# Value products two blocks of exponentials behind, and the side steps that move with them

## The chip, the cores and the metric

The kernel runs on one core of one Trainium2 chip. The metric is the device time of a launch in microseconds (us). The engines named below are TensorE (PE; its weight loads are PEld), VectorE (DVE), ScalarE (ACT), GpSimd (POOL) and SyncE (SP), which here only starts DMAs. Each engine works through its own list of instructions in order and waits on semaphores that others raise.

## The reference

The input x is 32 sequences of 128 rows by 512 columns, float32. The first layer is cross attention with 8 heads of 16 dimensions over the 512 columns, the second a mixture of experts.

```python
q = proj(x1t, Wq, bq); k = proj(x2t, Wk, bk); v = proj(x2t, Wv, bv)
scores = einsum('bhqd,bhkd->bhqk', q, k) / sqrt(D_HEAD)
attn = softmax(scores, axis=-1)
out = einsum('bhqk,bhkd->bhqd', attn, v)
x = x + tanh(g_xattn[0]) * xattn(layernorm(x), ctx)
# rmsnorm, router (8 experts, the best 2), gate/up/down of 256, one shared expert
x = x + tanh(g_ffn[0]) * ffn(layernorm(x))
```

## The kernel before, in words

One sequence, b, has 512 positions. For each of the 8 heads the 512 keys are cut into 4 tiles of 128, which gives 32 steps (STEPS) a sequence, each with a score tile of 128 keys by 512 queries. The attention stage is a loop over turns i = -3 to 31; each engine's list holds the same turns, and a turn has 32 steps in 8 blocks of 4 (GROUP). The order is written out by hand: constants such as PROJECT_AT, VALUES_LATE and LOGITS_AT (lines 35 to 43) say at which step a side job stands in each engine's list.

In turn i TensorE does, block by block (line 969 on): four matmuls of scores of sequence i+1 for the row maxima (max_scores, L838), which VectorE reduces two at a time (maximum, L1089, two pairs of PSUM banks); two score tiles of sequence i (exp_scores, L860); one group of four value products (values, eight matmuls in float32, L890); two more score tiles. ScalarE takes the exponential of each score tile (L1351) into one of three probs buffers of four tiles each. The score tiles, and also the projections, turned maxima, turned tokens and router logits, share three PSUM banks in rotation (take_bank): a bank's next user waits for the reader of its last content.

The value products of one sequence are eight groups r. Group r takes the probs of block r. Groups 0 to 3 add up in one PSUM bank, pv_ps, then ScalarE copies it out (take_values, L1366), and groups 4 to 7 add up in the same bank and are copied out as well. The product of a half's first group therefore waits for the copy of the half before (line 888). In the kernel before, group r is issued one block behind its exponentials: at step s, group s/4 - 1, and group 7 in the first block of the next turn. take_values stands at step VALUES_LATE + 1 = 4 (second half of sequence i-1) and 20 (first half of i) of ScalarE's list.

The copied bank holds numerators and the sums of exponentials (denominators). SyncE spreads the denominators over partitions (spread_denominators, L454), VectorE inverts them (invert, L1081, at step RECIP_AT), SyncE stores and reloads the reciprocals (L458, L464), and GpSimd multiplies, gates and adds to x (add_attention, L655 to L657). One turn later VectorE takes moments (moments2), GpSimd normalises into the single buffer tok (tokens, L676 to L690, which waits for the turning of the tokens before), and one more turn later TensorE turns it (turn_tokens, L865), ScalarE copies it (take_turned, L1373), and TensorE makes router logits (router_logits, L877). The negated row maxima go from ScalarE (take_maxima, L1358) by one DMA for each half into the q stack (row, L498), where the score tiles of that half need them.

After turn 31 come 103 jobs of the expert stage, which starts when TensorE's list has ended the attention.

Of the kernel before, what the change touches and what calls it, by code (L numbers as in the profile page):

```python
# [31 lines left out]
COLUMNS = tuple(slice(c, c + 2 * DH) for c in range(0, P, 2 * DH))  # L32
STEPS = HEADS * KT

PROJECT_AT = {24: (3, 0), 28: (3, 1), 8: (2, 2)}
EVAC_AT = {27: (3, 0), 31: (3, 1), 11: (2, 2)}
MAX_AT = (19, 3)
VALUES_LATE = 3
TURN_TOKENS_AT = 12
LOGITS_AT = 16  # L40
MOMENTS2_AT = 10
MOMENTS_AT = 27
RECIP_AT = 12
GROUP = 4
EXPERTS = 8
FF = 256
# [34 lines left out]
def build(nc, x_d, ctx_d, g_xattn_d, g_ffn_d, wq_d, bq_d, wk_d, bk_d, wv_d, bv_d, rms_d, router_d, w_d, out_d):  # L81
    B = x_d.shape[0]
# [5 lines left out]
    with es:  # L88
# [291 lines left out]
        def is_b(b):  # L380
            return 0 <= b < B
# [9 lines left out]
        def _(sp):  # L391
# [33 lines left out]
            def copy_parts(b, n, part):  # L425
                if part == HI:
                    if n == 0:
                        if b >= 3:
                            sp.wait_ge(s_es, STEPS * (b - 2))
                        if b < 3:  # L430
                            sp.wait_ge(s_blank[b], 1)
                    sp.wait_ge(s_hi, 2 * b + n + 1)
                if part == LOW:
                    sp.wait_ge(s_part, 2 * b + n + 1)
                stack, src = (k_stack, q_stack)[n][b % 3], parts[n][part]
                for at, slot in enumerate(SLOTS_OF[n]):
                    if slot == part:
                        for a in range(2):
                            rows = stack[LANE * a + at:LANE * a + at + STACK - 2:len(SLOTS_OF[n]), :, :]
                            sp.dma_start(rows.bitcast(F32), src[a:P:2, :].bitcast(F32)).then_inc(s_cp[n], DMA)  # L440
# [8 lines left out]
            def spread_denominators(b):  # L449
                sp.wait_ge(s_u, 2 * b + 2)  # L450
                if b:
                    sp.wait_ge(s_rc, b)
                for g in range(2):
                    sp.dma_start(den_c[P // 2 * g:P // 2 * (g + 1), :], pv_sb[1:P:2 * DH, g, :]).then_inc(s_sc, DMA)  # L454
# [40 lines left out]
            def row(b, half):  # L495
                sp.wait_ge(s_mr, 2 * b + half + 1)
                pairs = slice(half * GROUP // 2, (half + 1) * GROUP // 2)
                sp.dma_start(q_stack[b % 3][STACK:STACK + LANE + 1:LANE, pairs, :].bitcast(F32), m_rows[half].bitcast(F32)  # L498
                             ).then_inc(s_row[half], DMA)

            for i in TURNS:
                if is_b(i + 2):
                    copy_parts(i + 2, 0, HI)
                if is_b(i - 1):
                    spread_denominators(i - 1)
                if is_b(i):
                    row(i, 1)
                if is_b(i + 2):
                    copy_parts(i + 2, 0, LOW)
                if is_b(i - 1):  # L510
                    send_values(i - 1)
                if is_b(i + 2):
                    copy_parts(i + 2, 1, HI)
                if is_b(i - 1):
                    store_reciprocals(i - 1)
                if is_b(i + 2):
                    copy_parts(i + 2, 1, LOW)
                if is_b(i - 1):
                    load_reciprocals(i - 1)
                if is_b(i + 1):  # L520
                    row(i + 1, 0)
                if is_b(i + 4) and i + 4 >= 2:
                    load_ctx(i + 4)
                if is_b(i - 3):
                    store_turned(i - 3)
                if i >= 0 and is_b(i + X_AHEAD):
                    load_x(i + X_AHEAD)
                if is_b(i - 2):
                    store_tokens(i - 2)
                if i < 0:  # L530
                    load_x(i + X_AHEAD)
                if 0 <= i + 2 < len(STAGED):
                    store_staged(i + 2)
                if 0 <= i + 3 < len(STAGED):
                    load_staged(i + 3)
                for r in SHARED_ROWS.get(i, ()):
                    if r == 2:
                        sp.wait_ge(s_sst, DMA * len(STAGED))
                    if r == 0:
                        sp.wait_ge(s_wsh, (W_ROWS - 1) * DMA)  # L540
                    sp.dma_start(w_shared[:, r, :], w_d[0, :, r, :]).then_inc(s_wsh, DMA)
                if i == B - 2:
                    source(0)
                if i == -1:
                    sp.wait_ge(s_spare, 2)
                    map_tiles = map_d.rearrange("(n s) k -> n s k", s=P)
                    for n in range(0, EXPERTS * B, P):
                        sp.dma_start(map_tiles[n:n + P], slot_map[:]).then_inc(s_map0, DMA)
                    sp.dma_start(map_tiles[EXPERTS * B:], unused_map).then_inc(s_map0, DMA)
                if i == 0:  # L550
                    sp.dma_start(w_router[:], router_d.rearrange("(c p) e -> p c e", p=P)).then_inc(s_wnorm, DMA)
# [235 lines left out]
        def _(pe):  # L787
# [93 lines left out]
            def values(b, r):  # L881
                g, kt = divmod(r, KT)
                pair = 8 * b + r
                pe.wait_ge(s_exp, STEPS * b + GROUP * (r + 1))
                if r == 0:
                    pe.wait_ge(s_evac, 3 * b + 3)
                if kt == 0 and pair:
                    pe.wait_ge(s_u, pair // KT)
                for j in range(GROUP):
                    last = nc.tensor.matmul(pv_ps[2 * DH * j:2 * DH * (j + 1), :], v_ones[b % 3][:, kt, GROUP * g + j, :],  # L890
                                            probs[pair % 3][:, j, :], start=(kt == 0), stop=(kt == KT - 1))
                last.then_inc(s_pv, 1)
# [76 lines left out]
            for i in TURNS:  # L969
                for s in range(0, STEPS, GROUP):  # L970
                    if is_b(i + 1):
                        max_scores(i + 1, s)
                        max_scores(i + 1, s + 2)
                    if is_b(i):
                        exp_scores(i, s)
                        exp_scores(i, s + 1)
                    if s == 0 and is_b(i - 1):
                        values(i - 1, STEPS // GROUP - 1)
                    if s and is_b(i):
                        values(i, s // GROUP - 1)  # L980
                    if is_b(i):
                        exp_scores(i, s + 2)
                        exp_scores(i, s + 3)
                    if s + 3 == MAX_AT[1] and is_b(i):
                        turn_maxima(i, 1)
                    if s + 3 == MAX_AT[0] and is_b(i + 1):
                        turn_maxima(i + 1, 0)
                    if s == TURN_TOKENS_AT and is_b(i - 3):
                        turn_tokens(i - 3)
                    if s == LOGITS_AT and is_b(i - 3):  # L990
                        router_logits(i - 3)
                    if s in PROJECT_AT and is_b(i + PROJECT_AT[s][0]):
                        project(i + PROJECT_AT[s][0], PROJECT_AT[s][1])
                    if s + 3 == COUNT_SLOT and i > CHUNK and (i - 3) % CHUNK == 0:
                        count_choices((i - 3) // CHUNK - 1)
                    if i == B - 1 and s == FIRST_JOB_AT:
                        gate_up(0)

            values(B - 1, STEPS // GROUP - 1)

            for j in range(JOBS + 1):
                if j in ROUTER_JOBS:
# [19 lines left out]
        def _(dve):  # L1022
# [171 lines left out]
            for i in TURNS:  # L1194
                for s in range(STEPS):
                    if s % 2 == 0 and is_b(i + 1):
                        maximum(i + 1, s)
                    if s == RECIP_AT and is_b(i - 1):
                        invert(i - 1)
                    if s == MOMENTS_AT and is_b(i + 5):  # L1200
                        begun.append(moments(i + 5))
                    if s == MOMENTS2_AT and is_b(i - 2):
                        begun.append(moments2(i - 2))
                    if s == LOGITS_AT + 3 and is_b(i - 3):
                        take_logits(i - 3)
# [124 lines left out]
        def _(act_e):  # L1330
# [48 lines left out]
            for i in TURNS:  # L1379
# [3 lines left out]
                for s in range(STEPS):  # L1383
# [6 lines left out]
                    if s == EXP_SLOT and i > CHUNK and (i - 3) % CHUNK == 0:  # L1390
                        exponentials((i - 3) // CHUNK - 1)
                    if s == TURN_TOKENS_AT + 3 and is_b(i - 3):
                        take_turned(i - 3)
                    if s == VALUES_LATE + 1 and is_b(i - 1):
                        take_values(i - 1, 1)
                    if s == STEPS // 2 + VALUES_LATE + 1 and is_b(i):
                        take_values(i, 0)
                    if s in EVAC_AT and is_b(i + EVAC_AT[s][0]):
                        evacuate(i + EVAC_AT[s][0], EVAC_AT[s][1])

# [103 lines left out]
```

## Time and profile before

| | us |
|---|---|
| median of 3 runs (1446.69 to 1449.7) | 1448.16 |
| the profiled execution | 1446.75 |
| its span, first to last instruction | 1444.9 |
| TensorE busy | 1319.2 (91%) |
| VectorE busy | 889.8 (62%) |
| ScalarE busy | 853.4 (59%) |
| GpSimd busy | 730.8 (51%) |
| mean granted clock of TensorE, of full speed | 0.968 |

Busy time is the union of an engine's instructions; one that waits for nothing is no bound. Idle time is given beside the instruction that ended it and what released it. A row with xN merges N instructions that follow each other, so a wait inside such a row shows as a longer row and not as idle time. The starts and lengths of matmuls overlap by some hundredths of a us.

### The profile page before, as it was taken

The page shows a single profiled execution, that of the slowest core. Times are in us where ns is not written, and L with a number is a line of the kernel's source. Part 1 is how long each engine was busy: PE and PEld are TensorE (multiplying, and loading weights), DVE is VectorE, ACT ScalarE, POOL GpSimd, SP SyncE. Part 2 cuts the span into 40 slices and gives each one's busy share as a digit, 9 for nine tenths or more (in the row PEclk, how much of TensorE's full clock was granted, in tenths as well). Part 3 has the DMA queues.
Part 4 walks back from the last instruction along what each step waited for, and adds up shares of the span by engine and source line. Part 5 has one row for each costly group of instructions (what it writes and reads, how often), then busy time and mean ns, then how long its engine had stood idle before and what let it go on. Part 6 is the DMA issues. An engine that isn't in the chain of part 4 may idle for free.

```text
span 1444.9 us, 27029 instructions
## 1 busy us (share of the span) xinstructions
PE 1319.2 (91%) x9190; PEld 716.7 (50%) x9190; DVE 889.8 (62%) x1176; ACT 853.4 (59%) x1684; POOL 730.8 (51%) x978
## 2 busy tenths in 40 slices
PE   5989998998998998899999988899899999999997
PEld 2333333333333333333333333387678888888886
DVE  6777777777777778877777776256554333333332
ACT  1677777777777777777777776533234433333332
POOL 7445555545555555546776552120732555555553
PEclk7899999999999999999999998699999999999999
DMA  6555455545545544544665651164963898786665
GB/s 177 151 125 171 149 135 152 156 134 146 162 134 142 163 134 141 169 126 119 148 157 122 140 124 47 64 208 139 105 165 91 190 216 211 180 195 113 109 111 81
DMA packets 123841, 205.84 MB, mean 142 GB/s; under 512 B 28005, under 2 KB 29676, under 8 KB 123710
## 3 DMA queue, kind: packets, MB, share of 16 engines
q1 hardware_dynamic: 105454, 166.74, 42.9%
q0 software_dynamic: 18256, 37.38, 14.1%
q8 instruction: 79, 1.29, 0.4%
q14 instruction: 52, 0.43, 0.1%
HBM read 82.34 MB, written 61.94 MB: 100 GB/s over the span
## 4 chain that ended last, share of the span: by engine, by line
PE 72%; issue 9%; ACT 8%; DVE 4%; DMA 4%; POOL 2%; POOLq 1%; SPq 0%; ACTq 0%; DVEq 0%
PE m_banks L933 20%; PE bank L890 18%; PE bank L860 14%; PE m_banks L838 9%; ACT arena L1351 4%; PE bank L815 4%; PE bank L865 3%; DVE row_max L1089 2%; DMA arena<-ht_d 2%; PE bank L821 2%; ACT arena L1366 2%; POOL xs L757 1%; PE bank L955 1%; PE bank L877 1%; DMA out<-xs,arena 1%
## 5 line engine op out<-in xcount | busy, mean ns | idle before, releaser
L1089 DVE TENSOR_REDUCE row_max<-m_banks 128x2 f32<-128x1024 f32 x512 | 605.9, 1216 | 181.9 <-PE m_banks L838 181.0
L1351 ACT ACTIVATE arena<-bank 128x512 f32<-128x512 f32 x1024 | 557.1, 598 | 227.4 <-PE bank L860 226.5
L890 PE MATMUL bank<-arena 128*32 128x512 f32 x2048 | 284.0, 627 | 70.0 <-ACT arena L1366 68.8
L860 PE MATMUL bank<-q_stack,k_stack 49*128 49x512 f32 x1024 | 285.4, 472 | 2.2 <-ACT arena L1351 2.0
L860 PEld LDWEIGHTS bank<-q_stack,k_stack 49*128 49x128 f32 x1024 | 123.4, 189 | 277.9 <-issue 162.5
L838 PE MATMUL m_banks<-k_stack,q_stack 48*128 48x512 f32 x1024 | 195.9, 456 | 7.3 <-DVE row_max L1089 7.2
L769 POOL DMA_INDIRECT out<-xs,arena x71 | 112.6, 1586 | 159.8 <-ACT xs L1429 121.8
L933 PE MATMUL m_banks<-w_ring,h_hi 128*128 x568 | 183.1, 403 | 0.0
L1418 ACT ACTIVATE arena<-m_banks 128x256 f32<-128x256 f32 x103 | 39.5, 384 | 183.3 <-PE m_banks L933 183.3
L838 PEld LDWEIGHTS m_banks<-k_stack,q_stack 48*128 48x128 f32 x1024 | 90.2, 191 | 98.5 <-issue 68.0
L890 PEld LDWEIGHTS bank<-arena 128*32 128x32 f32 x2048 | 42.6, 109 | 156.2 <-ACT arena L1351 114.3
L933 PE MATMUL m_banks<-w_ring,h_lo 128*128 x284 | 111.7, 393 | 0.0
L933 PEld LDWEIGHTS m_banks<-w_ring,h_hi 128*128 128x128 f32 x568 | 101.4, 189 | 18.4
L1282 DVE TENSOR_TENSOR arena<-arena,m_banks 128x256 f32<-128x256 f32 x71 | 29.9, 421 | 115.7 <-ACT arena L1418 115.7
L712 POOL DMA_INDIRECT map_d<-meta,slots x64 | 64.5, 1008 | 64.8 <-DVE slots L1165 46.4
L1429 ACT ACTIVATE xs<-m_banks,arena 128x512 f32<-128x512 f32 x71 | 48.8, 687 | 71.0 <-PE m_banks L933 71.0
L678 POOL TENSOR_SCALAR arg<-mv 128x1 f32<-128x1 f32 x32 | 6.2, 192 | 166.1 <-DVE mv L1061 166.1
L1276 DVE TENSOR_TENSOR act_lo<-bank,act_hi 128x256 fp32r<-128x256 f32 x71 | 30.1, 424 | 96.6 <-ACT act_hi L1435 96.6
L933 PE MATMUL m_banks<-w_ring,act_hi 128*128 x284 | 87.5, 389 | 1.4 <-DVE act_lo L1276 1.4
L646 POOL CAST arena<-arena 128x512 fp32r<-128x512 f32 x62 | 37.8, 609 | 97.3 <-ACT arena L1338 96.4
L757 POOL DMA_INDIRECT xs<-h_d,arena x71 | 69.7, 981 | 33.3 <-issue 21.0
L815 PE MATMUL bank<-arena 128*32 128x512 f32 x512 | 72.8, 643 | 12.5 <-POOL arena L638 7.7
(175 smaller groups left out, 1795.0 us busy)
## 6 DMA issues: line engine op xcount, KB each, us to landing
k_stack<-arena SPq DMA_DIRECT2D x192, 128.0 KB
q_stack<-arena SPq DMA_DIRECT2D x192, 128.0 KB
split_d<-staged SPq DMA_DIRECT2D x30, 512.0 KB, 5.1
w_ring<-split_d SPq DMA_DIRECT2D x60, 256.0 KB
arena<-in_w SPq DMA_DIRECT2D x36, 256.0 KB, 7.5
arena<-in_ctx SPq DMA_DIRECT2D x32, 256.0 KB, 3.2
xs<-in_x SPq DMA_DIRECT2D x32, 256.0 KB, 4.0
arena<-arena SPq DMA_DIRECT2D x64, 128.0 KB, 3.2
```

The source lines that it names most:

```text
L712: nc.gpsimd.indirect_dma_start(map_d, bass.IndirectOffsetOnAxis(ap=slots[:, k, b:b + 1], axis=0), meta[:, k, b, :], None).then_inc(s_sc2, DMA)
L757: nc.gpsimd.indirect_dma_start(gathered[i % IN_RING], None, h_d, bass.IndirectOffsetOnAxis(ap=ids[:, i:i + 1], axis=0)).then_inc(s_got[i % ...
L769: nc.gpsimd.indirect_dma_start(out_d, bass.IndirectOffsetOnAxis(ap=ids[:, i:i + 1], axis=0), y_sb[i % OUT_RING], None, compute_op=ALU.add) ...
L815: last = nc.tensor.matmul(out[c, :], (wk, wq)[n][:, c], ctx_in[b % 2] if n == 0 else xn[b % 2], start=True, stop=True)
L838: nc.tensor.matmul(m_ps[pair % M_PAIRS][:, a, :], q_stack[b % 3][rows, h, qt * P:(qt + 1) * P], k_stack[b % 3][rows, h, :], start=True, st ...
L860: nc.tensor.matmul(out, k_stack[b % 3][rows, h, kt * P:(kt + 1) * P], q_stack[b % 3][rows, h, :], start=True, stop=True).then_inc(s_es, 1)
L865: last = nc.tensor.transpose(out[:, c * P:(c + 1) * P], src[:, c * P:(c + 1) * P], ident[:])
L890: last = nc.tensor.matmul(pv_ps[2 * DH * j:2 * DH * (j + 1), :], v_ones[b % 3][:, kt, GROUP * g + j, :], probs[pair % 3][:, j, :], start=( ...
L933: last = nc.tensor.matmul(out, v[:, c, :], weights(j, part, first_row + c), start=(c == 0 and n == 0), stop=(c == chunks - 1 and n == 2))
L1089: nc.vector.reduce_max(pair, m_ps[(STEPS * b + u) // 2 % M_PAIRS], AX_X).then_inc(s_mx, 1)
L1351: nc.scalar.activation(probs[group % 3][:, j, :], bank_of["scores", b, s], ACT.Exp, scale=float(DH) ** -0.5).then_inc(s_exp, 1)
L1429: nc.scalar.activation(y_sb[i % OUT_RING], Y_PS[j % 2], ACT.Copy, scale=wts[:, i:i + 1]).then_inc(s_yrt, 1)
```

## The change

The value products move from one block behind their exponentials to two: at step s of turn i TensorE issues group s/4 - 2, and in the first two blocks of a turn groups 6 and 7 of the sequence before. After the loop two groups are left instead of one. VALUES_LATE goes from 3 to 5, so take_values stands at steps 6 and 22. The third projection (values of sequence i+2) moves from step 8 to 12 and its evacuation from 11 to 15. The turned tokens go from step 12 to 4 (copied by ScalarE at 7 instead of 15), the router logits from 16 to 8 (copied by VectorE at 11 instead of 19). The reciprocals move from step 12 to 14. In SyncE's list the row of maxima of the second half goes ahead of the denominators.

```diff
--- before.py
+++ after.py
@@ -32,15 +32,15 @@
 COLUMNS = tuple(slice(c, c + 2 * DH) for c in range(0, P, 2 * DH))
 STEPS = HEADS * KT
 
-PROJECT_AT = {24: (3, 0), 28: (3, 1), 8: (2, 2)}
-EVAC_AT = {27: (3, 0), 31: (3, 1), 11: (2, 2)}
+PROJECT_AT = {24: (3, 0), 28: (3, 1), 12: (2, 2)}
+EVAC_AT = {27: (3, 0), 31: (3, 1), 15: (2, 2)}
 MAX_AT = (19, 3)
-VALUES_LATE = 3
-TURN_TOKENS_AT = 12
-LOGITS_AT = 16
+VALUES_LATE = 5
+TURN_TOKENS_AT = 4
+LOGITS_AT = 8
 MOMENTS2_AT = 10
 MOMENTS_AT = 27
-RECIP_AT = 12
+RECIP_AT = 14
 GROUP = 4
 EXPERTS = 8
 FF = 256
@@ -501,10 +501,10 @@
             for i in TURNS:
                 if is_b(i + 2):
                     copy_parts(i + 2, 0, HI)
+                if is_b(i):
+                    row(i, 1)
                 if is_b(i - 1):
                     spread_denominators(i - 1)
-                if is_b(i):
-                    row(i, 1)
                 if is_b(i + 2):
                     copy_parts(i + 2, 0, LOW)
                 if is_b(i - 1):
@@ -974,10 +974,10 @@
                     if is_b(i):
                         exp_scores(i, s)
                         exp_scores(i, s + 1)
-                    if s == 0 and is_b(i - 1):
-                        values(i - 1, STEPS // GROUP - 1)
-                    if s and is_b(i):
-                        values(i, s // GROUP - 1)
+                    if s < 2 * GROUP and is_b(i - 1):
+                        values(i - 1, STEPS // GROUP - 2 + s // GROUP)
+                    if s >= 2 * GROUP and is_b(i):
+                        values(i, s // GROUP - 2)
                     if is_b(i):
                         exp_scores(i, s + 2)
                         exp_scores(i, s + 3)
@@ -996,7 +996,8 @@
                     if i == B - 1 and s == FIRST_JOB_AT:
                         gate_up(0)
 
-            values(B - 1, STEPS // GROUP - 1)
+            for r in range(STEPS // GROUP - 2, STEPS // GROUP):
+                values(B - 1, r)
 
             for j in range(JOBS + 1):
                 if j in ROUTER_JOBS:
```

## Rows read from the trace of the kernel before

**Rows 1.** The page, parts 1 and 2: busy time, and TensorE's clock

```profile
PE 1319.2 (91%) x9190; PEld 716.7 (50%) x9190; DVE 889.8 (62%) x1176; ACT 853.4 (59%) x1684; POOL 730.8 (51%) x978
...
PEclk7899999999999999999999998699999999999999
```

**Rows 2.** Waits of the whole span: us in total, times, longest us

```profile
PE bank L890 <- ACT arena L1366: 68.8, 63, 1.3
...
PE bank L877 <- ACT arena L1351: 10.0, 28, 0.4
```

**Rows 3.** Windows: busy time of each engine over four turns, then clock, DMA

```profile
323.00:432.20 109.20, 98.81 (x866) 38.12 (x864) 82.66 (x89) 83.26 (x160) 62.49 (x96) 1.00 0.52 147
```

**Rows 4.** Timeline, TensorE, one turn: start, length, what, idle before

```profile
500.69 1.06 PE L815 MATMUL bank<-arena 128*32 128x512 f32 x8
...
505.01 0.73 PE L838 MATMUL m_banks<-k_stack,q_stack 48*128 48x512 f32 x4
505.58 0.40 PE L860 MATMUL bank<-q_stack,k_stack 49*128 49x512 f32 x2
505.91 1.07 PE L890 MATMUL bank<-arena 128*32 128x512 f32 x8
...
508.33 0.73 PE L860 MATMUL bank<-q_stack,k_stack 49*128 49x512 f32 x2
510.05 1.07 PE L890 MATMUL bank<-arena 128*32 128x512 f32 x8 [0.99 <-ACT arena L1366]
...
511.86 0.87 PE L860 MATMUL bank<-q_stack,k_stack 49*128 49x512 f32 x2
512.72 1.07 PE L890 MATMUL bank<-arena 128*32 128x512 f32 x8
...
521.32 0.44 PE L877 MATMUL bank<-w_router,arena 128*32 128x8 f32 x32 [0.36 <-ACT arena L1351]
...
523.90 1.06 PE L890 MATMUL bank<-arena 128*32 128x512 f32 x8 [1.25 <-ACT arena L1366]
...
525.70 0.88 PE L860 MATMUL bank<-q_stack,k_stack 49*128 49x512 f32 x2
...
527.99 1.06 PE L815 MATMUL bank<-arena 128*32 128x512 f32 x8
528.99 0.73 PE L838 MATMUL m_banks<-k_stack,q_stack 48*128 48x512 f32 x4
```

**Rows 5.** Timeline of ScalarE in the same turn

```profile
509.33 0.58 ACT L1366 COPY arena<-bank 128x512 f32<-128x512 f32 x1
...
511.58 2.06 ACT L1351 ACTIVATE arena<-bank 128x512 f32<-128x512 f32 x4 [1.17 <-PE bank L860]
...
518.55 0.59 ACT L1373 COPY arena<-bank 128x512 f32<-128x512 f32 x1
```

**Rows 6.** Timeline of TensorE around a fall of the clock

```profile
666.01 1.57 PE L890 MATMUL bank<-arena 128*32 128x512 f32 x8 [1.25 <-ACT arena L1366]
...
673.74 0.73 PE L838 MATMUL m_banks<-k_stack,q_stack 48*128 48x512 f32 x4
```

**Rows 7.** Timeline of TensorE in the last two turns

```profile
885.13 1.93 PE L890 MATMUL bank<-arena 128*32 128x512 f32 x8 [1.25 <-ACT arena L1366]
...
896.80 1.06 PE L890 MATMUL bank<-arena 128*32 128x512 f32 x8
...
900.95 1.07 PE L890 MATMUL bank<-arena 128*32 128x512 f32 x8 [0.98 <-ACT arena L1366]
...
928.65 1.07 PE L890 MATMUL bank<-arena 128*32 128x512 f32 x8
```

**Rows 8.** Timelines of SyncE's queue and VectorE, last turn: denominators

```profile
900.83 1.16 SPq L454 DMA_DIRECT2D arena<-arena  x2
...
903.28 0.35 DVE L1081 RECIPROCAL arena<-arena 128x32 f32<-128x32 f32 x1 [5.25 <-issue]
```

**Rows 9.** Timeline of GpSimd in the turn of rows 4: attention is added

```profile
524.20 1.28 POOL L655 TENSOR_TENSOR arena<-arena 128x512 f32<-128x512 f32 x1 [1.42 <-DMA arena<-rden_d]
```

## The prediction

> **What bounds the kernel now.** I read the page first. TensorE is busy 91% of the span and every other engine 62% or less, and its clock is at full speed in nearly all slices [rows 1]. The edit touches only the attention stage, so the next view is a window of four turns there: of 109.2 us TensorE works 98.8, ScalarE 83.3, VectorE 82.7 and GpSimd 62.5 [rows 3]. That is 27.3 us a turn, the same as from one first half of a key projection to the next, 500.69 to 527.99 [rows 4]. TensorE stands idle 2.6 us of it, and the list of waits says for what: 68.8 us in 63 waits of the value products for ScalarE's copy of the bank of products (L1366), and 10.0 us in 28 waits of the router logits for an exponential [rows 2]. In the timeline these are 0.99 us ahead of group 0, 1.25 ahead of group 4 and 0.36 ahead of the logits [rows 4]. The stage is thus bound by TensorE's list with two places a turn at which the list runs through ScalarE: last products of a half, an exponential that stands ahead in ScalarE's list, the copy, the next products.
>
> A third cost hangs on these waits. The granted clock falls from 2.4 to 1.2 GHz five times in the attention stage behind its start, and all five times within a wait for the copy, or at the products right behind it: ahead of the products that begin at 113.2, 621.8, 666.0, 885.1 and 900.9 us. The same eight products then last 1.57 to 1.93 us and not 1.07 [rows 4, 6, 7].
>
> **The change part by part.** The work of TensorE, ScalarE and VectorE stays the same, instruction for instruction; only places change. So the sum is the old turn, less the waits that go, plus those that appear.
>
> *The waits for the copy.* With two blocks of distance, group 7 stands in block 1 of the next turn and group 0 in block 2, and the copy stands behind exponential 6. I wrote the turn out from its first maxima (time 0; 505.01 before). Steps from rows: maxima to scores 0.57, scores to products 0.33, products 1.0 to the next scores, scores to what follows 0.43 where no bank is late [rows 4]; an exponential 0.515 (four in 2.06) and a copy 0.58 [rows 5]. Group 7 runs at 4.0 to 5.0, scores 6 and 7 end at 5.45, exponential 6 ends at 6.0, the copy at 6.55. Turned tokens (about 0.6) and four maxima stand between, so that group 0 can't be reached before 6.95. The 0.99 is gone. At group 4 there is no such filler: exponential 22 ends at about 18.7, the copy at 19.25, and the products would be reached at 19.1. With the 0.14 from the end of the copy to the products seen before (509.91 to 510.05 [rows 4, 5]), 0.25 to 0.3 of the 1.25 is left.
>
> *The wait of the logits (0.36).* At step 8 the logits stand behind scores 10 and 11, and their bank's last reader, exponential 9, ends at 8.6, with the logits reached at 8.8. It goes.
>
> *Banks that come late.* Three banks are shared, so TensorE is never more than three uses ahead of the readers. Before, this shows as score rows of 0.73, 0.87 and 0.88 us in place of 0.40 [rows 4]. After, the first stays. In block 2 scores 9 need exponential 7, which stands behind the copy: it ends at 7.0 where the scores could start at 6.6, 0.45 lost (0.47 before). ScalarE then also has the turned tokens in the same stretch (0.59 [rows 5]), which costs 0.2 in block 3. In block 5 scores 21 wait 0.3 for exponential 19, which takes the place of most of the 0.48 before. Together about 0.1 to 0.2 more than before; with the 0.3 of group 4 the new waits are 0.4.
>
> The turn is then 27.3 - 2.6 + 0.4 = 25.1 us, 2.2 less. For turns 1 to 29 that is 29 x 2.2 = 63.8. Turn 0 has only the second of the two waits: 0.9. Turn 30 gives 2.2, turn 31 about 1.8 by its two waits (0.98 and the like [rows 7]). Sum 68.7.
>
> *Value projection at step 12, reciprocals at step 14, row ahead of denominators.* The projection (about 1.0) fits anywhere: its bank reader stands three steps behind as before, and group 0 of that sequence comes two turns later. The queue of SyncE now has: row of maxima at about 3.9, denominators at 6.6, low parts of k, numerators, high parts of q, then it waits for the reciprocals (12.8), with low parts of q and the reload (16.2, as it waits for the store; 3.4 in the old turn) behind. The low parts of q land near 18 and are needed at 25.1. The denominators have 5.9 us until the inversion; in the last turn before they needed 2.45 (900.83 to 903.28, where VectorE waited for them alone [rows 8]). The attention is then added from about 19.8, which is 0.6 later in the turn than 524.20 less 505.01 [rows 4, 9], and GpSimd is free at 23.1, with the next split due at 22.6. That lateness of 0.5 meets a need that is two us off, at the next turn's start. I cost all this at nothing; if the cover went, every us of lateness would be one us a turn.
>
> *VectorE.* Two reductions a block need 2.4 us (82.7 us over four turns, 20.7 a turn, with all side steps [rows 3]); blocks without side work become 2.66. It fits, with 0.3 to spare. In the three or four turns with routing steps it will not: +2 in all, bounds 0 to 5.
>
> *The clock.* Where the waits go, the falls should go. In the middle of the stage a fall costs 7.73 (666.01 to 673.74 [rows 6]) against 5.09 for the same work (523.90 to 528.99 [rows 4]): 2.64, twice, and some 1.1 for the shorter first one: 6.4. In turn 30 three steps of groups took 11.67 (885.13 to 896.80 [rows 7]) against three times 2.67 (510.05 to 512.72 [rows 4]): 3.7. In turn 31 six steps took 27.7 (900.95 to 928.65 [rows 7]). At full clock ScalarE would bound them: 24 exponentials 12.4, copies 1.1, the first job's products some 3, gaps 1.6: about 18, so 9.6 at stake. But that turn has no maxima, TensorE idles in small pieces of 0.3 a block, and the clock stayed low there while TensorE was busy throughout. Bounds 0 and 9.6. I take 4.8, as the nearest rows (a fall in turn 30 that lasted half a turn) are a fall later than now.
>
> **Sum.** 1446.75 (the profiled execution's own time) - 68.7 - 6.4 - 3.7 - 4.8 + 2 = 1365.2. The median before is 1.4 above that execution; I don't add it. The end of the stage is neutral: group 7 of the last sequence waits for the last exponential as before, with group 6 now in that wait. The expert stage is untouched. **1365 us.**
>
> **The rivals.**
> - *ScalarE takes the place.* Idle times of 1.17 us follow each of its copies, elsewhere 0.6 at most [rows 5]. If these only shrink to 0.6, and the rest of its waits for score tiles stay, the turn is 27.3 - 2 x 0.57 = 26.2, and the time 1365 + 30 x 1.1 = 1398. For it speaks that copy and turned tokens now meet in two blocks; against it that ScalarE has 20.8 us of work in 25.1 [rows 3].
> - *Only TensorE's own work is left*, because the late banks vanish too: another 0.8 a turn, 1340.
> - *The wait only moves.* The copy has to follow group 7 and precede group 0 in any order, so at group 0 and 4 a wait of the same size could stand: 1446, within 0.2%. Against it: the list has a whole block between them where it had half of one.
> - *Slower: the clock stays low.* The small waits for banks remain, in every turn, at full density of work. A whole turn at 1.2 GHz costs about 13 us, by three steps of groups 3.7 dearer [rows 4, 7], scaled to eight steps and the denser projections. From 7 turns on it eats the gain; at 8 the time is 1365 + 104 = 1469. Against it: no fall stood at a late bank alone, five of five at the copy. The Trainium skill has the rule that speaks for it: in "TensorE: Matmul & The Clock Gate", section "A second HAM failure mode: psum-queue depth-cycling", a kernel that cycles through PSUM banks idles briefly so often that the clock swings between its two levels. The trace of before agrees only for the long waits.
>
> **How the numbers follow.** Forecast 0.68 (its own range 1355 to 1380: turn 31's clock is 5 either way, 0.2 us a turn another 6, routing turns 3). ScalarE 0.17, only TensorE's work 0.08, the wait moves 0.03, slower 0.04. The range for 8 in 10 is 1350 to 1396: all of the first, half of the second, a third of the third. Faster by over 0.2% (about what a measurement of this kernel can tell from no change) 0.93, within 0.2% 0.03, slower 0.04.
>
> **What would show it.** Right: waits of the value products for L1366 fall from 68.8 to under 12, only ahead of group 4; the logits' 10.0 is near 0; the distance of two key projections is 25.1; long score rows remain in blocks 1, 2, 3 and 5; no clock fall between 100 and 800 us; the inversion waits for nothing. Wrong: score rows of 1 us or more, exponentials back to back over a whole block (then ScalarE bounds), maxima that wait for VectorE in ordinary turns, k or q copies awaited at a turn's start, or falls of the clock at places without a wait for the copy.

## The result and the profile after

The kernel after runs in 1382.83 us (median of 4 runs, 1377.97 to 1384.4), the kernel before beside it in 1448.93. The ratio is 0.954, with an interval of 0.9514 to 0.9567. The profiled execution took 1382.71 us, with a span of 1380.9; the prediction was 1365, so 66 us were gained where 84 were forecast.

The page of the kernel after, parts 1 and 2 (against rows 1):

```profile
PE 1323.4 (96%) x9190; PEld 714.6 (52%) x9190; DVE 886.5 (64%) x1176; ACT 855.2 (62%) x1684; POOL 733.8 (53%) x978
...
PEclk7799999999999999999999999999999999999999
```

A window of 109.2 us in the attention stage of the kernel after, with the columns of [rows 3]:

```profile
300.00:409.20 109.20, 107.97 (x904) 40.91 (x902) 88.06 (x94) 89.01 (x171) 65.76 (x104) 1.00 0.51 150
```

TensorE is now idle for 1.2 us in 109.2, where it was 10.4 [rows 3]. The list of waits of the kernel after has no line any more for the value products behind the copy, which led [rows 2], nor one for the logits behind an exponential. What is left, with a line of GpSimd that grew from 71.1 us before:

```profile
POOL arena L655 <- DMA arena<-rden_d: 142.1, 28, 14.5
...
PE bank L860 <- ACT arena L1352: 8.6, 36, 0.5
```

The timeline of TensorE in an ordinary turn of the kernel after, from the first maxima of the turn (columns as in rows 4):

```profile
425.81 0.73 PE L838 MATMUL m_banks<-k_stack,q_stack 48*128 48x512 f32 x4
...
429.12 0.75 PE L860 MATMUL bank<-q_stack,k_stack 49*128 49x512 f32 x2
429.80 1.07 PE L890 MATMUL bank<-arena 128*32 128x512 f32 x8
...
432.38 0.39 PE L860 MATMUL bank<-q_stack,k_stack 49*128 49x512 f32 x1
432.96 0.50 PE L860 MATMUL bank<-q_stack,k_stack 49*128 49x512 f32 x1 [0.19 <-ACT arena L1352]
433.38 1.06 PE L890 MATMUL bank<-arena 128*32 128x512 f32 x8
...
435.74 0.80 PE L860 MATMUL bank<-q_stack,k_stack 49*128 49x512 f32 x2
436.47 1.06 PE L890 MATMUL bank<-arena 128*32 128x512 f32 x8
...
442.23 0.76 PE L860 MATMUL bank<-q_stack,k_stack 49*128 49x512 f32 x2
442.91 1.06 PE L890 MATMUL bank<-arena 128*32 128x512 f32 x8
...
444.88 0.71 PE L860 MATMUL bank<-q_stack,k_stack 49*128 49x512 f32 x2
445.66 1.06 PE L890 MATMUL bank<-arena 128*32 128x512 f32 x8
...
451.39 0.73 PE L838 MATMUL m_banks<-k_stack,q_stack 48*128 48x512 f32 x4
```

The turn is 25.58 us (425.81 to 451.39) against 27.3. Group 0 (433.38) and group 4 (445.66) wait for nothing that is listed. But from the start of the scores to the products it takes 0.68, 1.00, 0.73, 0.68 and 0.78 us at these five places (the blocks of groups 7, 0, 1, 3 and 4), where it takes 0.33 if no bank is late [rows 4]. ScalarE in the same turn shows why the second is the longest:

```profile
431.82 0.58 ACT L1367 COPY arena<-bank 128x512 f32<-128x512 f32 x1
432.29 0.62 ACT L1352 ACTIVATE arena<-bank 128x512 f32<-128x512 f32 x1
432.77 0.61 ACT L1374 COPY arena<-bank 128x512 f32<-128x512 f32 x1
433.24 1.13 ACT L1352 ACTIVATE arena<-bank 128x512 f32<-128x512 f32 x2
```

The copy of the products, exponential 7, the copy of the turned tokens and exponentials 8 and 9 follow each other without a gap: two copies in a stretch with the usual four exponentials.

Summed over the turns, measured between the turned maxima at each turn's start: turn 0 is 2.0 us longer; turns 1 to 28 gain 54.4 (48.2 is 28 times 1.72, the rest falls of the clock and routing turns); turn 29 gains nothing (26.14 after 26.00); turn 30 gains 3.9, turn 31 9.3; the expert stage takes 514.6 in place of 512.6. With 0.6 ahead of turn 0 that is the 64 us by which the span fell.

### The profile page after: what moved, and what is told of

Same layout as the page of the kernel before. It is cut to its first block, busy times and chain, and to the rows that moved or that the text cites. A ratio compares the mean times of both kernels' runs of the same rounds, so it can differ in the third digit from the quotient of the medians.

```text
span 1380.9 us, 27056 instructions
## 1 busy us (share of the span) xinstructions
PE 1323.4 (96%) x9190; PEld 714.6 (52%) x9190; DVE 886.5 (64%) x1176; ACT 855.2 (62%) x1684; POOL 733.8 (53%) x978
## 4 chain that ended last, share of the span: by engine, by line
PE 69%; issue 13%; POOL 5%; DMA 4%; DVE 4%; ACT 2%; POOLq 1%; SPq 1%; ACTq 0%; DVEq 0%
PE bank L890 18%; PE bank L860 16%; PE m_banks L933 15%; PE m_banks L838 11%; PE bank L815 4%; DVE row_max L1090 2%; POOL map_d L712 2%; PE bank L821 2%; POOL xs L757 2%; ACT arena L1352 2%; DMA out<-xs,arena 2%; PE bank L847 1%; PE bank L865 1%; PE bank L877 1%; PE bank L955 1%
## 5 line engine op out<-in xcount | busy, mean ns | idle before, releaser
L860 PE MATMUL bank<-q_stack,k_stack 49*128 49x512 f32 x1024 | 294.0, 466 | 10.3 <-ACT arena L1352 8.6
L890 PE MATMUL bank<-arena 128*32 128x512 f32 x2048 | 275.5, 610 | 2.3 <-ACT arena L1352 0.2
L838 PE MATMUL m_banks<-k_stack,q_stack 48*128 48x512 f32 x1024 | 204.7, 468 | 8.7 <-DVE row_max L1090 8.5
L838 PEld LDWEIGHTS m_banks<-k_stack,q_stack 48*128 48x128 f32 x1024 | 87.4, 189 | 114.3 <-issue 73.5
L655 POOL TENSOR_TENSOR arena<-arena 128x512 f32<-128x512 f32 x32 | 41.0, 1282 | 153.6 <-DMA arena<-rden_d 142.1
L757 POOL DMA_INDIRECT xs<-h_d,arena x71 | 69.7, 982 | 32.8 <-issue 21.0
L815 PE MATMUL bank<-arena 128*32 128x512 f32 x512 | 71.9, 635 | 11.8 <-POOL arena L638 7.0
L648 POOL TENSOR_TENSOR arena<-arena 128x512 fp32r<-128x512 f32 x62 | 79.3, 1278 | 5.0
```

Of the source, the lines that this page charges most:

```text
L648: nc.gpsimd.tensor_tensor(lo, proj[n], hi.bitcast(F32), ALU.subtract).then_inc(s_part, 1)
L757: nc.gpsimd.indirect_dma_start(gathered[i % IN_RING], None, h_d, bass.IndirectOffsetOnAxis(ap=ids[:, i:i + 1], axis=0)).then_inc(s_got[i % ...
L815: last = nc.tensor.matmul(out[c, :], (wk, wq)[n][:, c], ctx_in[b % 2] if n == 0 else xn[b % 2], start=True, stop=True)
L838: nc.tensor.matmul(m_ps[pair % M_PAIRS][:, a, :], q_stack[b % 3][rows, h, qt * P:(qt + 1) * P], k_stack[b % 3][rows, h, :], start=True, st ...
L860: nc.tensor.matmul(out, k_stack[b % 3][rows, h, kt * P:(kt + 1) * P], q_stack[b % 3][rows, h, :], start=True, stop=True).then_inc(s_es, 1)
```

## The experiments

Two theories stood against each other at first: A, that the distance between the last products of one half and the first of the next brings the gain; B, that the moved side steps bring it. All turns named below are ordinary ones, 4 to 16 or so, whose length repeats within some hundredths of a us in one execution, except where the clock falls. The times of e1, e2, e3, e7, e8 and e9 are of one run each; where a ratio is given, it is of four runs or more against the kernel before on the same chip.

**e1: the distance alone.** The kernel before with

```diff
-VALUES_LATE = 3
+VALUES_LATE = 5
-                    if s == 0 and is_b(i - 1):
-                        values(i - 1, STEPS // GROUP - 1)
-                    if s and is_b(i):
-                        values(i, s // GROUP - 1)
+                    if s < 2 * GROUP and is_b(i - 1):
+                        values(i - 1, STEPS // GROUP - 2 + s // GROUP)
+                    if s >= 2 * GROUP and is_b(i):
+                        values(i, s // GROUP - 2)
```

and both last groups behind the loop.

> The kernel before with the two blocks of distance and the copies at steps 6 and 22, all side steps where they were. Theory A (the distance between the last products of a half and the first of the next brings the gain): the waits of the value products for the copy, 68.8 us before, fall under 12; the wait of the logits (about 0.35 a turn) stays, as they stand behind the turned tokens as before; an ordinary turn is 25.9 us (27.3 before, 25.6 after), the time about 1392. Theory B (the moved side steps bring it, the distance only moves the wait): the turn stays at 27 or more, the time above 1435.

It took 1381.76 us, with a turn of 25.10: shorter than the 25.58 of the whole change, and shorter than expected. Theory B fell. TensorE in such a turn of e1 has the logits' wait of before, one for VectorE, and fewer late banks. The third row is a single long wait in turn 23, and the fourth, of VectorE, shows what stood behind it:

```profile
408.90 0.44 PE L877 MATMUL bank<-w_router,arena 128*32 128x8 f32 x32 [0.36 <-ACT arena L1352]
...
412.25 0.50 PE L838 MATMUL m_banks<-k_stack,q_stack 48*128 48x512 f32 x2 [0.35 <-DVE row_max L1090]
...
642.18 0.80 PE L838 MATMUL m_banks<-k_stack,q_stack 48*128 48x512 f32 x2 [3.64 <-DVE row_max L1090]
```

```profile
640.70 0.35 DVE L1082 RECIPROCAL arena<-arena 128x32 f32<-128x32 f32 x1 [3.61 <-DMA arena<-arena]
```

The inversion stood in VectorE's list ahead of the reductions and waited for the transfer of the denominators, which SyncE had issued at 633.00. That is the cover which the prediction costed at nothing. Here, with the inversion two steps earlier than in the change, it failed twice in full turns, by 3.6 and 1.0 us, and turn 23 took 32.8 us; the change has no such wait. Three waits for the DMA of the row of maxima took 4.5 us more, so that the time is no better than the change's.

**e2: the side steps alone.** The kernel after with the one-block value products and VALUES_LATE = 3 of before.

> The kernel after with one block of distance and the copies at steps 4 and 20 again, the side steps at their new places. Theory A: both waits for the copy are back at about 1.0 and 1.25 us, the turn is 27.0 (the logits' 0.36 gone), the time about 1437, and the clock falls again at waits for the copy. Theory B: the turn is near 25.6, the time under 1395.

1432.25 us, a turn of 27.05, waits for the copy of 59.4 us in 63. As theory A has it, except that the second wait is 0.91 and not 1.25. The clock fell at seven of the 63, five of them between 80 and 520 us, each of these five at products that had waited 0.90 to 0.99 us for the copy, as here:

```profile
510.17 1.94 PE L890 MATMUL bank<-arena 128*32 128x512 f32 x8 [0.98 <-ACT arena L1366]
```

**e3: the copy one step up, nothing else.**

```diff
-VALUES_LATE = 3
+VALUES_LATE = 2
```

> The kernel before with the copies one step up in ScalarE's list (behind exponentials 3 and 19), nothing else. Theory A says that the wait is made of what stands ahead of the copy in ScalarE's list, so each wait shortens by one exponential, 0.5 us: the turn is 26.3, the waits for the copy sum to about 37 us, the clock falls less often, the time 1405 to 1415. Rival (the wait is the copy's own length and the semaphores): the waits stay at 1.0 and 1.25, the time stays within 3 us of before.

1383.28 us (before on that chip: 1444.83) with a turn of 25.60: about the same as the whole change, by one constant. I had expected half of it. Group 0 waits 0.49 in place of 0.99, as expected. Group 4 waits for nothing, and ScalarE shows why. In e3, with TensorE's rows around them:

```profile
407.76 1.07 PE L890 MATMUL bank<-arena 128*32 128x512 f32 x8 [0.49 <-ACT arena L1366]
...
419.06 0.44 PE L877 MATMUL bank<-w_router,arena 128*32 128x8 f32 x32 [0.35 <-ACT arena L1351]
...
420.33 1.07 PE L890 MATMUL bank<-arena 128*32 128x512 f32 x8
```

```profile
419.54 0.56 ACT L1366 COPY arena<-bank 128x512 f32<-128x512 f32 x1
420.43 1.08 ACT L1351 ACTIVATE arena<-bank 128x512 f32<-128x512 f32 x2 [0.34 <-PE bank L860]
```

In the kernel before, the copy stood behind exponential 20, whose score tile only came after the logits; ScalarE idled, then did the exponential, then the copy. One step up, the copy fills that idle time and is over at 420.1, before the products are reached at 420.33. The wait was not made of work but of the copy's place behind an exponential that itself waited for TensorE.

**e12: e3 again, with six runs.**

> The kernel of e3 (before, with VALUES_LATE 2 in place of 3) again, timed in rounds. Its one run was at 1383.28. If the turn of 25.6 us is all that counts, the ratio to before is 0.953 to 0.960, not told from the whole change's 0.954; if its single run was a lucky one, 0.965 or more.

Ratio 0.9628 (0.9604 to 0.9652), between the two expectations; its turn is again 25.60. The chip of this pair of runs was another, and before took 1492.63 us on it. There, turns 26 to 29 took 35, 33, 29 and 29 us where VectorE waited for something outside the program's own queues. So e3 equals the change in its ordinary turns and nearly in its one time; on a chip with other disturbances its ratio stays 0.9 of a per cent behind, and I can't say whether the change's would, too, as it was not run there.

**e4: fill the wait.** The kernel before with

```diff
-PROJECT_AT = {24: (3, 0), 28: (3, 1), 8: (2, 2)}
-EVAC_AT = {27: (3, 0), 31: (3, 1), 11: (2, 2)}
+PROJECT_AT = {16: (3, 0), 28: (3, 1), 0: (2, 2)}
+EVAC_AT = {19: (3, 0), 31: (3, 1), 3: (2, 2)}
```

> The kernel before, one block of distance, but with two of the three projections moved into the blocks right ahead of the waits (value projection at step 0 in place of 8, key projection at 16 in place of 24), about 1.0 us of work each. If the wait only needs something in front of it, 2.0 us a turn go: the turn is 25.3 to 25.6 and the time 1380 to 1390, as good as the change without the longer distance. Rival: with one block of distance ScalarE is the limit, the new block order makes the products wait for exponentials, and the turn is 26.3 or more, the time above 1405.

1479.49 us, ratio 1.0228 (1.0176 to 1.0279), a turn of 28.4: slower than before where a gain was expected. TensorE and, in the second fence, ScalarE:

```profile
414.76 1.08 PE L821 MATMUL bank<-arena 128*32 128x128 f32 x32 [0.36 <-ACT arena L1351]
...
417.99 1.07 PE L890 MATMUL bank<-arena 128*32 128x512 f32 x8 [1.25 <-ACT arena L1366]
```

```profile
416.77 0.60 ACT L1351 ACTIVATE arena<-bank 128x512 f32<-128x512 f32 x1 [0.26 <-PE bank L860]
417.27 0.58 ACT L1366 COPY arena<-bank 128x512 f32<-128x512 f32 x1
```

The filler delays not only the products but also score tile 4, behind whose exponential the copy stands. The wait at group 0, shown here, grew from 0.99 to 1.25, the one at group 4 stayed at 1.25, and the projection's own bank wait of 0.36 comes on top. From these rows I infer that a filler helps only where it lies between the tile that the copy stands behind and the products. In the kernel after, the turned tokens lie there; in e4 the projections lie ahead of both. No run has a filler at that place with one block of distance, so this is not shown. The 63 waits of e4 (77.8 us) also say how seldom such a wait lowers the clock: it fell at two of them, both in the last two turns.

**e7: the copy two steps up** (VALUES_LATE = 1, else the kernel before).

> The kernel before with the copies two steps up (behind exponentials 2 and 18). One step up left 0.49 us at group 0 and nothing at group 4. Theory A: the last 0.49 goes, the turn is 25.1 (25.6 with one step), the time about 1370, with the old block distance of one. Rival: the copy now stands where it waits for the last products themselves, ScalarE idles, the exponentials behind it come late and the turn is no shorter than 25.6.

1396.49 us, a turn of 25.70. The rival holds, by a somewhat other way: the copy no longer delays the products, but it stands ahead of exponential 3, whose bank score tile 5 needs:

```profile
405.27 0.40 PE L860 MATMUL bank<-q_stack,k_stack 49*128 49x512 f32 x1
406.00 0.49 PE L860 MATMUL bank<-q_stack,k_stack 49*128 49x512 f32 x1 [0.34 <-ACT arena L1351]
```

That the time is 13 us above e3's with a turn only 0.1 longer lies mainly in turn 31, where the clock fell at 850.9 and stayed low until 878.2. No wait of 1 us stood ahead of it, only short ones:

```profile
849.47 0.49 PE L860 MATMUL bank<-q_stack,k_stack 49*128 49x512 f32 x1 [0.36 <-ACT arena L1351]
850.44 0.49 PE L860 MATMUL bank<-q_stack,k_stack 49*128 49x512 f32 x1 [0.49 <-ACT arena L1351]
850.87 1.93 PE L890 MATMUL bank<-arena 128*32 128x512 f32 x8
```

**e5: distance, and the row of maxima of the second half ahead of the denominators** (e1 with that part of the change).

> The two blocks of distance and the row of maxima ahead of the denominators in SyncE's list, nothing else of the change (side steps and reciprocals where they were). The distance alone gave an ordinary turn of 25.10 us but lost the gain to single waits, three of them for a late row of maxima (4.5 us and one turn of 32.8). Theory A: the row ahead of the denominators is what takes these away; the turn stays 25.1, no wait for the DMA of q_stack is left, the time is 1364 to 1370, below the full change. Theory B: those waits come from the load on the DMA queues and not from the order; they stay, and the time is 1378 or more.

1373.06 us, ratio 0.9513 (0.9461 to 0.9566), the turn 25.10. Less than e1's single time, but not by the reason given: two waits for a row (3.7 us) are left of three (4.5). What went is the one long turn, in which the inversion had waited for the denominators; they are issued behind the row here, so the order did not help them. I don't claim the row's place as a gain of this change; e11 below tests the other row.

**e9: the change with its side steps back** (e5 with RECIP_AT = 14).

> The change with only the side steps (turned tokens, logits, value projection) where they were before; distance, copies at 6 and 22, reciprocals at 14 and the row of maxima ahead stay. If the moved side steps cost the 0.5 us a turn by which the change (25.59) is behind the distance with the row ahead (25.10), this one is at 25.10 and at 1370 to 1377. If the later reciprocals cost it, it is at 25.5 or more and at 1382 or more.

1374.38 us, the turn 25.10. So the later reciprocals are free and the moved side steps cost 0.49 us a turn, though they do away with the logits' wait. Over 28 turns that is 14 us. The one time here shows 8 of it: turn 20, turn 30 and all from turn 31 on are 1.1, 1.0 and 2.1 us longer than the change's, and three turns gain nothing. Where the 0.49 lies can be read by halves. From the first to the second turned maxima of a turn the change takes 13.12 us and e9 12.27; 0.37 of the difference is the logits, which stand in this half in the change alone. The other half is 12.47 against 12.84, the same 0.37 the other way. So the whole loss lies in the half in which the copy of the products and that of the turned tokens meet.

**e6: one side step to a block** (the change with the value projection at step 4, turned tokens at 8, logits at 12).

> The change, but with the side steps spread one to a block: value projection at step 4, turned tokens at 8, logits at 12. Theory A (the turned tokens' copy right behind the copy of the products holds back ScalarE and with it the shared banks, 0.5 us a turn; the logits' wait is gone where ScalarE is not late): the turn is 24.6 to 25.2, the time 1350 to 1370. Rival (the total of ScalarE's work and the three banks set 25.6, wherever the side steps stand): 25.5 or more, the time 1378 or more.

1377.39 us, ratio 0.9544 (0.9486 to 0.9602), the turn 25.32 in place of 25.59. Half of the loss comes back: the place of the turned tokens matters, but neither theory's number was met, and by its ratio the kernel can't be told from the change. Two copies meet here as well, as the one of the projection now stands at step 7. But the projection keeps TensorE busy for 1.01 us where the turned tokens take 0.59, and from the next scores to the products it is 0.57 and not 1.00.

**e8: the change with its copies two steps later** (VALUES_LATE = 7).

> The change, but with the copies two steps later (behind exponentials 8 and 24), so that they again have too little room ahead of the next products. Theory A: waits of 1.0 to 1.3 us for the copy are back twice a turn, the turn is 27.5 to 28, and the clock falls again at some of these waits between 100 and 800 us (none there in the change): time 1440 to 1455. If the falls have another cause (the turn's place or the data), none is seen there and the time is at most 27.8 a turn, about 1440.

1437.65 us. The waits are back, 67.3 us in 63, 1.05 or so each, and the turn is 27.2; it and the time are a little below the expectation. The clock falls three times between 80 and 800 us, each time at such a wait or right behind it. The products behind one, at half the clock:

```profile
253.64 1.94 PE L890 MATMUL bank<-arena 128*32 128x512 f32 x8 [1.05 <-ACT arena L1367]
```

**e10: the copies in ScalarE's gap** (e5 with VALUES_LATE = 4, behind exponentials 5 and 21).

> Two blocks of distance, row of maxima ahead, side steps and reciprocals as before, and the copies one step up, behind exponentials 5 and 21, where ScalarE idles about 0.6 us until the next score tile. Theory (what a copy costs is set by whether it runs in a gap of ScalarE or ahead of an exponential whose bank is waited for): the score rows of 0.72 behind group 7 shorten to about 0.45, the turn is 24.7 to 24.8 (25.10 with the copies at 6 and 22), the time 1360 to 1366. Rival (the place of the copy no longer matters once the products don't wait for it): 25.1 and 1370 to 1375. A copy that waits for the products itself would give 25.4 or more.

1366.33 us, ratio 0.9439 (0.9396 to 0.9482), the lowest of all, yet with a turn of 25.05. The theory of the gap failed here: the score rows ahead of group 0 did not shorten, as the copy now waited for the products itself:

```profile
424.03 0.59 ACT L1367 COPY arena<-bank 128x512 f32<-128x512 f32 x1 [0.21 <-PE bank L890]
```

The turns account for only 1.4 of the 7 us to e5; the two profiled executions are 2.9 apart and the ranges of the two ratios overlap, so the rest is not placed. The largest wait left is at the start of turn 30, with a fall of the clock behind it:

```profile
801.93 0.79 PE L860 MATMUL bank<-q_stack,k_stack 49*128 49x512 f32 x2 [2.05 <-DMA q_stack<-arena]
```

**e11: also the row of the first half ahead**, of the reload of the reciprocals.

```diff
+                if is_b(i + 1):
+                    row(i + 1, 0)
                 if is_b(i - 1):
                     load_reciprocals(i - 1)
-                if is_b(i + 1):
-                    row(i + 1, 0)
```

> The kernel of e10 with, in SyncE's list, also the row of maxima of the first half ahead of the reload of the reciprocals. In e10 one wait of 2.05 us for that row, at the start of turn 30, is left, and the clock falls right behind it from 801 to 814 us; the row stood behind a reload that itself waited for the store to land. If the order is the cause, the row leaves some 2 us earlier, wait and fall go, and the time falls by 5 to 8 us to 1358 to 1361, the turn staying 25.05. If the load on the DMA engines there is the cause (the shared expert's weights are loaded then), the wait stays and the time is 1364 to 1370.

1407.02 us on the chip on which before took 1492.63: ratio 0.9438 (0.9408 to 0.9467), no other than e10's. The waits for rows are gone from the trace, none is listed, and so is the fall at that place; turn 30 is 22.9 us against 26.0 in e10. The row now leaves 1.0 us behind the copies of q and not 3.8, and this 2.8 is more than the wait of 2.05: the order is enough to account for it. It is not the only thing that differs, though. On this chip TensorE was held up in turns 26 to 28, and the row had 11.2 us until its scores where it had 4.0 in e10; the order gives 2.8 of that. The gain of 5 to 8 us that I expected is not shown. The chip's own disturbances look like this on VectorE, three times, with a "remote" releaser that is no queue of the program:

```profile
722.99 0.17 DVE L1075 COPY arena<-bank 128x8 f32<-128x8 f32 x1 [6.30 <-remote]
```

## Why the prediction was right, and by how much it was off

**The waits for the copy and for the logits.** Right. 2.6 us a turn went, as summed from the two waits and the logits' [rows 4]; e1 and e2 show that the distance takes the first two and the side steps the third. e3 adds what the prediction did not see: with one block of distance, the copy's place alone takes the second whole and half of the first. Nothing of the 0.3 at group 4 is listed as a wait, though the products at 445.66 begin 0.15 behind the end of the copy (444.93 to 445.51), as they did before; most of it lies inside the long score row ahead.

**The late banks.** This term was mis-sized, and it is most of the miss. The forecast had 0.4 us of new waits a turn; 27.3 less 2.6 is 24.7, and 25.6 was measured, so they are 0.9. By place, from the rows above, over the undisturbed 0.33: 0.35, 0.67, 0.40, 0.35 and 0.45 at the blocks of groups 7, 0, 1, 3 and 4, where I had 0.35, 0.45, 0.2, 0.3 and 0.3. That is 2.2 in place of 1.6. Added up over a turn, and the old waits left out, the score rows take 0.6 to 0.7 more than before; the rest is in the rows of maxima, which take 4.8 us in place of 4.5 and for which I had put nothing. The main step that failed is the one in blocks 2 and 3. I had seen that the two copies meet on ScalarE, and took the cost as the excess of one block instead of letting it run on into the next. e9 shows that the moved side steps cause it, and in which half: with them back the turn is 25.10, by chance the number that was forecast. 0.49 x 28 is 14 of the 18 us by which the forecast missed.

**The clock.** Right in kind. Five falls in the attention stage became one, and none stands between 60 and 800 us. e2 and e8 bring waits of about 1 us back and falls with them; e3, with waits for the copy of 0.49 at most, has none behind the stage's start. But most waits of that size bring no fall, 58 of 63 before and 61 of 63 in e4, so which of them does is not explained. In turn 31 I took half of 9.6 us, and the clock stayed up: 24.8 us from the turned maxima (841.45) to the turned tokens (866.24), 34.1 before. That was in part luck. Of the ten profiles in which no wait of over 0.6 us stands in the first 20 us of that turn, nine took 24.4 to 25.1 us, but e7 35.0. The rule of the Trainium skill that I weighed ("TensorE: Matmul & The Clock Gate", the section on depth-cycling) would have the clock swing under brief idle times from cycling through banks. In the full turns it did not: with 2.2 us of late banks in every turn the granted clock is 1.00 in the window above. The fall of e7 in turn 31, behind waits of 0.36 and 0.49 for a bank, is the one place that agrees with it.

**Turn 30.** 5.9 us were forecast for it (a wait pair and the clock) and 2.2 for turn 29; 3.9 and nothing came. The SyncE and TensorE rows of the kernel after:

```profile
807.01 0.58 SPq L498 DMA_DIRECT2D q_stack<-arena  x1
```

```profile
814.09 0.50 PE L860 MATMUL bank<-q_stack,k_stack 49*128 49x512 f32 x2 [1.60 <-DMA q_stack<-arena]
814.52 1.22 PE L890 MATMUL bank<-arena 128*32 128x512 f32 x8
...
818.50 1.93 PE L890 MATMUL bank<-arena 128*32 128x512 f32 x8
```

The row of maxima was issued at 807.01 and let TensorE go at 814.09, and the clock fell 1.2 us later, until 822. The wait lies just ahead of the turned maxima by which the turns are cut, so it takes turn 29's gain, and most of the fall lies in turn 30; e3, without the wait, took 24.35 and 23.63 us for the two where the change took 26.14 and 25.05. I had put SyncE's queue at nothing for an ordinary turn, which held, but had not looked at the turns in which shared weights are loaded. A shorter turn moves the first row's need up, and a reload that waits for its store stood ahead of it. In e11, without that order, the wait is gone. The 7.1 us from issue to release are long as well, and how much of them is the load of those turns stays open.

**GpSimd.** The attention is added 21.3 us into the turn, not 19.8 (the high parts of q took 3.7 us to issue, not 2.5), and its idle time ahead of that grew from 71.1 to 142.1 us. As forecast, no one waited for it.

**The small terms.** Turn 0 lost 2.0 in place of gaining 0.9. That need not be an effect of the order: one and the same kernel had 28.16 us there in e3 and 25.39 in e12. The expert stage lost 2.0 us, with the same order of instructions; its cause stays open. Against the forecast of 1365.2 for the profiled execution, 17.5 us are missing. Turns 1 to 28 lack 13.4 by their length, turn 29 lacks 2.3, turn 0 2.9, turn 30 2.0 and the expert stage 2.0; turn 31 gave 2.7 more than forecast, the other falls and the routing turns 1.8 more, and the start 0.6. So errors of 5 us the other way hid a part of the miss, which is luck.

**The rivals.** "ScalarE takes the place" was nearly as close as the forecast: it had 26.2 a turn and 1398 us, and what was measured lies between the two. Its reason was wrong (ScalarE's idle times behind the two copies are 0.54 and 0.19 in the turn above, not 0.6 each), its place (two copies in two blocks) right. The wait did not just move, and the clock did not stay low.

## What to carry to other kernels

Where one engine copies out what another accumulates, first look at what stands ahead of the copy in its engine's list: an item that itself waits for the other engine's next output turned a copy of 0.58 us into a wait of 1.25. Moving the copy one place (e3) took as much from an ordinary turn as the whole change with its deeper pipeline. Filler work ahead of the item that the copy stands behind only delays both (e4). Side steps that put two copies close together on the copying engine can hold up the shared banks for more than one block (e9). A single wait of about 1 us in a busy TensorE can cost some more us by the clock, here at 2 to 7 of 63 waits, so the waits are worth more than their sum.

## What the runs showed of the hardware

These are counts from the attention stage behind its first 60 us. The clock of TensorE fell behind single waits of 0.8 to 1.25 us although the engine was busy about 90% of the turn around them, at 5 of the 63 waits for the copy before, 7 of 63 in e2, 4 of 63 in e8 and 2 of 63 in e4. At each of the thirteen waits of 1.6 us or more, over all profiles, it fell during the wait or within 2 us of its end. Behind the many of 0.5 us it did not fall, with one exception: in turn 31 of e7 it fell behind two short waits, of 0.36 and 0.49, that stood 0.5 us apart.

Once low it stayed so for 3 to 14 us in full turns, but for 24 us in turn 31 of the kernel before and 27 in e7's. TensorE was busy for 22.2 of those 24 us, nearly all of it with score tiles and value products; the four products that turn tokens and the router logits in between did not raise the clock. A copy of a 128x512 bank by ScalarE took 0.58 us and a following exponential began 0.47 us after its start, so what it adds is 0.1 us less than its length. One chip gave 3 to 4% longer times than the others, for the kernel before (1492.6 us against 1441 to 1449), for e3's kernel (1433.0 against 1383.3) and for e11, which is close to e10 (1407.0 against 1366.3).
